# Splitting a tile's sums over keys around part of the value projection, in a decoder layer on one core

## The reference

```
q, k, v = x @ Wq.T + bq, x @ Wk.T + bk, x @ Wv.T + bv      # then softmax over heads, token by token
x1 = layernorm(x + att @ Wo.T + bo)
ig, fg = gates of [x1, ctx, ctx]                           # 16 heads
D  = exp(log_D - max(log_D)), lower triangle only
C  = (x1_h @ ctx_h.T) / sqrt(32) * D                       # per head h, 128 x 128
n  = max(|sum over keys of C|, exp(-max_log_D))
h  = (C / (n + eps)) @ ctx_h                               # the sums over keys, per head
x2 = layernorm(x1 + headwise_norm(h) * ln_scale)
x3 = layernorm(gated low-rank update of x2)
```

## Time and profile before

| | |
|---|---|
| median of 3 runs | 2005.21 us |
| profiled execution | 2007.69 us |
| its span | 2006.2 us |
| PE busy | 1854.5 us (92%) |
| weight loads busy | 1536.5 us (77%) |
| DVE busy | 1551.2 us (77%) |
| ACT / GpSimd (POOL) busy | 778.7 / 774.0 us (39% each) |
| mean granted TensorE clock | 0.936 of full speed |

### The profile page before, as it was taken

How to read it: one execution, slowest core, us unless ns; L and a number is a source line. 1 busy time by engine, 2 the same in 40 slices (tenths; PEclk the granted TensorE clock), 3 DMA queues, 4 the chain that set the end, 5 groups by cost and what they waited for, 6 DMA issues and landing times.

```text
span 2006.2 us, 67466 instructions
## 1 busy us (share of the span) xinstructions
PE 1854.5 (92%) x27656; PEld 1536.5 (77%) x27656; DVE 1551.2 (77%) x3898; ACT 778.7 (39%) x2193; POOL 774.0 (39%) x779
## 2 busy tenths in 40 slices
PE   0889999999999999999999999999999999999985
PEld 0678888887887887788788878878878877887863
DVE  4456777888878788887888888777887788887776
ACT  1223344344434434443443444344344344344341
POOL 1124344344334334433433443343344344344342
PEclk9988898999989999999999999899998999999895
DMA  4111122212221221211222122212212212221110
GB/s 137 59 65 55 65 65 76 75 65 77 79 74 58 78 74 63 79 71 64 75 79 74 63 79 77 75 58 78 74 63 74 74 63 74 74 83 58 63 54 27
DMA packets 53829, 141.14 MB, mean 70 GB/s; under 512 B 8767, under 2 KB 10431, under 8 KB 45578
## 3 DMA queue, kind: packets, MB, share of 16 engines
q1 hardware_dynamic: 53770, 140.31, 20.4%
HBM read 122.98 MB, written 17.30 MB: 70 GB/s over the span
## 4 chain that ended last, share of the span: by engine, by line
PE 83%; DVE 6%; ACT 6%; issue 3%; SPq 1%; POOL 0%; DMA 0%; POOLq 0%; ACTq 0%; DVEq 0%
PE bank L477 13%; PE bank L355 13%; PE bank L356 13%; PE bank L358 12%; PE bank L347 8%; PE quad L467 4%; PE bank L434 3%; PE bank L446 3%; PE bank L491 3%; PE bank L503 3%; PE bank L448 3%; PE bank L351 2%; ACT x_high L563 2%; DVE x L931 1%; ACT gs L599 1%
## 5 line engine op out<-in xcount | busy, mean ns | idle before, releaser
L713 POOL TENSOR_TENSOR ex<-ex,w_rec 128x512 f32<-128x512 f32 x64 | 67.6, 1056 | 766.5 <-DVE w_rec L827 766.5
L621 ACT ACTIVATE Dx<-Mb,a_col 128x128 f32<-128x128 f32 x1024 | 312.8, 395 | 0.0
L725 POOL TENSOR_TENSOR h_rs<-h_ve,half_neg 128x16 f32<-128x16 f32 x64 | 201.3, 3146 | 220.9 <-DVE h_ve L913 220.9
L477 PE MATMUL bank<-c,Dx 128*128 128x33 f32 x2048 | 270.3, 295 | 16.5 <-ACT LT L651 14.5
L477 PEld LDWEIGHTS bank<-c,Dx 128*128 128x128 f32 x2048 | 262.9, 211 | 23.8 <-ACT LT L651 21.5
L594 ACT ACTIVATE x1T<-bank 128x512 f32<-128x512 f32 x64 | 38.3, 598 | 356.1 <-PE bank L347 356.1
L892 DVE SCALAR_TENSOR_TENSOR Dx<-quad,Dx 128x512 f32<-128x512 f32 x256 | 159.0, 683 | 11.4 <-PE quad L467 2.8
L739 POOL TENSOR_TENSOR rs<-ve,half_neg 128x1 f32<-128x1 f32 x192 | 106.0, 552 | 153.3 <-DVE ve L848 153.2
L718 POOL TENSOR_SCALAR_AFFINE_SELECT Dx<-Dx 128x512 f32<-128x512 f32 x256 | 160.1, 638 | 5.5 <-ACT Dx L621 5.5
L355 PE MATMUL bank<-wv_high,x_high 128*128 128x512 f32 x256 | 151.0, 590 | 0.0
L347 PE MATMUL bank<-id_sb,x 128*128 128x128 f32 x512 | 85.3, 290 | 54.9 <-DVE x2sq L933 53.0
(11 more groups left out here) (157 smaller groups left out, 4551.4 us busy)
## 6 DMA issues: line engine op xcount, KB each, us to landing
Mb<-m_rows SPq DMA_DIRECT2D x64, 1024.0 KB, 4.6
xb<-in_x SPq DMA_DIRECT2D x256, 64.0 KB
xr<-in_x SPq DMA_DIRECT2D x64, 256.0 KB, 2.6
cb<-in_ctx SPq DMA_DIRECT2D x64, 256.0 KB, 3.6
out_dram<-yo SPq DMA_DIRECT2D x64, 256.0 KB, 2.4
Dx<-in_wq SPq DMA_DIRECT2D x4, 256.0 KB, 4.7
Dx<-in_wk SPq DMA_DIRECT2D x4, 256.0 KB, 5.5
Mb<-in_wv SPq DMA_DIRECT2D x4, 256.0 KB, 6.2
```

Of the source, the lines that this page charges most:

```text
L477: last = mm(bank[6 + h // 8][:, (h % 8) * HD:(h % 8 + 1) * HD], Dx[t.parity()][:, h % 4, h // 4, :], c1[:, h, :], start=True, stop=True)
L621: last = go(Dx[t.parity()][:, j, n, :], Mb[t.parity()][:, h, :], ACT.Exp, bias=a_col[t.parity()][:, h:h + 1], scale=-1.0)
L725: tt(h_rs[:], h_ve[:], half_neg[:], ALU.pow).then_inc(s.hrs_sb, 1)
```

## The change

The 16 sums over keys of tile `d` are issued in two parts. After the first five heads, PE issues the bias matmul and the first four of the eight high matmuls (chunks 0 and 1) of the value projection of tile `b`; then the other eleven heads, which raise `H_ps` at the end; then the last four high matmuls and the four low ones, which raise `v_ps`. The waits stay where they were, ahead of the first head and ahead of the bias. Where there is no tile `b` (the last two tiles of sums), the eleven heads follow the five at once.

```diff
+            def high_part(b, high, n, lo, hi):
+                for c in range(lo, hi):
+                    mm(bank[b][:], high[:, c, :], w_high[n][:, c, :], start=False, stop=False)
+                    mm(bank[b][:], high[:, c, :], w_low[n][:, c, :], start=False, stop=False)
+
+            def low_part(b, low, n):
+                for c in range(CH):
+                    last = mm(bank[b][:], low[:, c, :], w_high[n][:, c, :], start=False, stop=c == CH - 1)
+                return last
...
             def p_v(t):
                 edge(pe, t, (s.xhigh_sb, 0), (s.xlow_sb, 0), (s.VG_sb, 1), (s.QT_sb, 0), (s.fn1_sb, 4))
                 bias(4, 2)
-                product(4, x_high, x_low, 2, False).then_inc(s.v_ps, 1)
+                high_part(4, x_high, 2, 0, 2)
+
+            def p_v_rest(t):
+                high_part(4, x_high, 2, 2, CH)
+                low_part(4, x_low, 2).then_inc(s.v_ps, 1)
...
-                for h in range(H):
+
+            def heads(t, lo, hi):
+                for h in range(lo, hi):
                     last = mm(bank[6 + h // 8][:, (h % 8) * HD:(h % 8 + 1) * HD], Dx[t.parity()][:, h % 4, h // 4, :],
                               c1[:, h, :], start=True, stop=True)
-                last.then_inc(s.H_ps, 1)
+                return last
...
                 if d.real():
                     m_H(d)
+                    heads(d, 0, 5)
                 if b.real():
                     p_v(b)
+                if d.real():
+                    heads(d, 5, H).then_inc(s.H_ps, 1)
+                if b.real():
+                    p_v_rest(b)
                     m_cT(b)
```

## The result

The changed kernel takes 1921.03 us (median of 3 runs, 1920.44 to 1923.55), against 2005.21 us before. The ratio is 0.957, with a 95% interval of 0.951 to 0.963: 4.3% faster. 1926 us were forecast, with a range of 1910 to 1960.

What follows compares the result with a forecast made beforehand. PE's list of work bounds the kernel, slowed by clock falls behind the sums. Span 2006.2 - 66.4 (steady tiles) - 13 (first eight tiles) = 1926.8; + 1.5 - 2.5 = 1925.8, given as 1926 us, range 1910 to 1960.

Steps and rivals of the forecast that it cites:

- Where the time was: In 53 steady tiles, PE's low-clock stretches all begin at or behind the sums over keys; removing them is worth -66.4 us.
- That both kinds would go: The split of the sums removes every clock fall in the 53 steady tiles, -66.4 us; 0 if neither sort goes.
- early kind: Clock falls 1.4 to 1.9 us after the first sum, behind the scores and 6 to 8 heads; 9 of 53 tiles.
- late kind: Clock falls 3.4 to 4.3 us after the first sum, when all sums are done back to back; 24 of 53 tiles.
- The first eight tiles: Start of the program, 251.5 us at a clock of 0.89: -13 us, with ends of 0 and -26.
- The last tiles: End of the program, 85.3 us at 0.67, last two tiles of sums not split: 0 us, 5 either way.
- The seams: Two added wide-to-narrow changes on PE in each of 62 tiles: taken as 0 us, between -6 and +12.
- Sums that come later: Heads 5 to 15 end 1.15 us later, raising H_ps later: 0 us, or +19 us if the cover is gone.
- The rule on idle gaps: Trainium skill's rule that idle gaps between matmul bursts lower the clock; by it 2005 us instead of 1926.
- Half a cure: Eleven heads in a row still lower the clock behind the sums: about 1975 to 1985 us, chance 0.08.
- Nothing: The clock follows idle gaps or falls periodically whatever PE does: 2005 us, up to 2015, chance 0.06.
- Slower: Each of two narrow runs can lower the clock, slowing wide work between: 2022 to 2034 or 2110 us, chance 0.04.

Runs made afterwards that it cites:

- 8 and 8: The changed kernel with the sums split after head 8 in place of head 5: 1955.0 us, ratio 0.972.
- 2 and 14: The changed kernel with the sums split after head 2 in place of head 5: 1966.5 us, ratio 0.978.
- the run with the wide work first: The changed kernel with the bias and four high matmuls ahead of the first head and all 16 heads unbroken: 2025.1 us, ratio 1.000.
- the run with the work added between: The changed kernel with five unread wide matmuls between head 5 and head 6, the value projection whole behind the sums: 2150.7 us, ratio 1.058.
- the doubled columns: The kernel before, its 16 heads unbroken, each but the last streaming 66 columns in place of 33: 1926.6 us, ratio 0.957.

## Why the prediction was right

- **Where the time was.** The forecast rested on low stretches behind the sums and nowhere else in the steady part. All 33 are gone: 1494.0 - 1559.9 = -65.9 us, against -66.4.
- **That both kinds would go.** Right, and shown to hang on both sides of the split: 8 and 8 brings back falls of the early kind, 2 and 14 the late one. Five is between them. The wide work must also be enough: with one matmul in place of five the late kind stays.
- **The first eight tiles.** 251.5 became 230.8 us: -20.7, where I took -13 out of 0 to -26. This is the term that was mis-sized, and it is nearly all of the difference between 1926.8 and 1919.0 us of span. Before, eight of the nine low stretches in these tiles began behind the sums or among them, and one at a gap in the second tiled block. I had counted the gap inside the sums as a cause. After the change it is still there, 1.16 us long, and the clock stays at 1.00:

```profile
140.94 1.08 PE L493 MATMUL bank<-c,Dx 128*128 128x33 f32 x9 [1.16 <-issue]
```

  One low stretch is left at each of two places; the windows of these:

```profile
122.85:126.26 3.41, 3.41 (x8) 2.65 (x9) 1.29 (x2) 3.38 (x11) 1.34 (x2) 0.50 0.29 110
180.88:184.29 3.41, 3.41 (x10) 2.66 (x9) 3.13 (x9) 3.41 (x13) 1.91 (x3) 0.50 0.40 124
```

  Both stand behind the second tiled block with gaps in it (1.98 us before the first, 0.40 and 0.32 before the second). I had left half of the 26.1 us to gaps; 5.4 are left. Of these, 3.9 are PE's idle time above 1.05 us a tile (230.82 - 218.56 - 8 x 1.05) and 1.4 are work at the lower level (218.56 - 8 x 27.14).
- **The last tiles.** 85.3 became 84.7 us, as forecast.
- **The seams.** 28.19 us a tile against 28.17 to 28.19 before: at most 0.02 us for both, at the lower end of 0 to 0.10 each.
- **Sums that come later.** The last sum ends 4.83 us after the first starts (1019.02 + 2.54 - 1016.73), before 3.76: 1.07 us later. The copy starts 0.88 us later, since it had stood 0.2 us behind other work of ACT before. PE's wait for x2 is 53.0 us, as before, so the cover was there and nothing reached PE.
- **The range.** The ends that the prediction lists add up to 1902 and 1975 us, not to 1910 and 1950; it does not say how it put them together. The result lies inside either.
- **The rule on idle gaps.** In this kernel the clock fell on a PE that was busy, and held when only the streamed columns of the same matmuls changed. The other half of what the Trainium skill says in "TensorE: Matmul & The Clock Gate", section "Why this matters for your kernels", that an idle gap between bursts brings the clock down, does agree with the run with the wide work first, where the clock falls in each of the six gaps of 3.5 to 3.9 us. In the run with the work added between, low stretches also follow gaps of 2.0 to 2.7 us, shorter than those that the section warns of.
- **The rivals.** *Half a cure*, the early kind gone and the late one left, is what the same split with only the bias between gives (1978.0 us, where 1975 to 1985 were named), and 2 and 14 too (1966.5); 8 and 8 is the other half (1955.0). *Nothing* is ruled out by the doubled columns: the order and the pace are the old ones, and the falls are gone. *Slower* did not come: in the changed kernel the second run never pulled the clock down. In the 8 and 8 split the low stretch spans the second run and lasts 10.2 us, which fits its mechanism.

What stays open: every tile of the kernel before has the same unbroken run, yet 20 of 53 show no fall, and what decides this the runs do not show. Which split is best was not searched. The issue gaps of the run with the wide work first came without a longer program, and why is not known.

## What to carry to other kernels

Where PE is "busy" all the time, ask for the granted clock stage by stage before looking for waits. Here the price of narrow matmuls was paid by the wide ones behind them, so the line that looked slow (L355 with wv) was not the cause. In this kernel two cures cost nothing, since the weight loads set the pace of the narrow matmuls (the loads are busy for all 3.52 us of them, and twice the columns take no longer). One is to put wide work among them, enough of it; when choosing the place, count the scores ahead of them too. The other is to let each stream more columns in the time it takes anyway. Once the clock holds, look at the waits again: here the next one was worth another 0.68 us a tile. Whether it would have been worth as much at the old clock was not tested.

## What the runs showed of the hardware that was not expected

- Matmuls of 66 f32 columns on a 128 x 128 weight tile take the time of those with 33: 3.60 us for 16 heads to the bias in both. The clock falls with the one and holds with the other.
- A gap of 1.16 us inside the sums left the clock at 1.00, and 3.5 us of unbroken sums, with PE busy throughout, were followed by 0.50.
- Ten more matmuls in a loop body of two tiles brought instruction packets from 42 to 277 and a gap of 2.0 to 2.7 us on PE in every pass. A mere reordering brought 96 and six gaps of up to 3.9 us. The reorderings of the other runs left it at 42. So whoever adds or moves matmuls in this loop must look at that queue before he reads the time.
- Low stretches that hold sums are longer: 3.4 us where the fall came behind all sums, 6.8 us in the early kind, with half of the heads or more in it, and 10.2 us in the 8 and 8 split. That the sums at the lower level are what lengthens it is an inference.
